# The last attention written out head by head, its projection inside, and maxima passes over four key segments of 256

## The reference

```
qkv  = x @ qkv_w + qkv_b                       # 12 heads of 16 channels, 2 images: 24 heads in all
attn = (q * scale) @ k.T + rel_h + rel_w       # 2304 x 2304 scores per head
out  = softmax(attn) @ v
return out @ proj_w + proj_b
```

## Time and profile before

| | us |
|---|---|
| median of 3 runs | 4721.52 (4720.76 to 4724.44) |
| the profiled execution, its own time | 4717.87 |
| its span in the profile | 4716.0 |
| PE, PE weight loads, DVE, ACT, POOL busy | 3464.0, 1758.2, 3572.9, 2692.4, 1536.5 |
| first and last score of the last attention start | 3309.2 and 4642.6 |
| first maxima pass | 3245.9 |
| first projection matmul | 4678.7 |

### The profile page before, as it was taken

One profiled execution on the slowest core, in us unless ns is written; L12 is line 12 of the kernel. 1 busy time (PEld: TensorE's weight loads), 2 busy tenths in 40 slices (PEclk: granted clock), 3 DMA queues, 4 the chain that ended last, 5 costly groups with the idle time before them and its releaser, 6 DMA issues. The chain is left out here.

```text
span 4716.0 us, 120406 instructions
## 1 busy us (share of the span) xinstructions
PE 3464.0 (73%) x47313; PEld 1758.2 (37%) x47313; DVE 3572.9 (76%) x3605; ACT 2692.4 (57%) x4414; POOL 1536.5 (33%) x1124
## 2 busy tenths in 40 slices
PE   3898764148777756306777775765999999999996
PEld 2476622012222223101222222451566665666563
DVE  2755455869999936677999993555888888888884
ACT  0366617735555532864545542141888888888883
POOL 0122200059999920007999990000000000000000
PEclk8899977558888878656878887865999999999998
DMA  3433212432222220232222212133112222211213
GB/s 85 97 68 65 39 42 62 120 94 68 61 65 68 57 66 17 89 118 76 71 61 63 65 48 64 59 120 91 52 52 60 57 56 54 55 52 52 52 53 88
DMA packets 165533, 316.14 MB, mean 67 GB/s; under 512 B 71035, under 2 KB 110147, under 8 KB 161392
## 3 DMA queue, kind: packets, MB, share of 16 engines
q1 hardware_dynamic: 164976, 308.38, 24.9%
HBM read 199.70 MB, written 108.02 MB: 65 GB/s over the span
## 5 line engine op out<-in xcount | busy, mean ns | idle before, releaser
L2005 DVE TENSOR_REDUCE l3a_mx<-l3a_mx 128x2 f32<-128x768 f32 x1362 | 1223.9, 951 | 201.9 <-PE l3a_mx L1909 195.5
L1981 ACT ACTIVATE l3a_p<-l3a_s 128x384 f32<-128x384 f32 x2592 | 1158.5, 491 | 159.7 <-PE l3a_s L1931 149.6
L1398 POOL TENSOR_TENSOR l_scan_sc<-l_scan_s,l_scan_repc 128x768 f32<-128x768 f32 x576 | 1032.3, 1840 | 5.8 <-DVE l_scan_s L1376 5.7
L1335 ACT ACTIVATE l_scan_da<-l_scan_da,l_scan_a 128x768 f32<-128x768 f32 x576 | 504.0, 875 | 637.0 <-PE l_scan_da L1259 636.8
L1931 PE MATMUL l3a_s<-l3a_q,l3a_k 125*32 125x384 f16 x10368 | 827.7, 327 | 3.3 <-issue 3.3
L1909 PE MATMUL l3a_mx<-l3a_k,l3a_q 124*32 124x384 f16 x10896 | 717.0, 335 | 36.3 <-DVE l3a_mx L2005 29.4
L1259 PE MATMUL l_scan_dup<-l_scan_du,l_scan_pick 96*128 96x512 bf16 (+1 forms) x1152 | 350.7, 393 | 367.4 <-DMA l_scan_dt<-l_dtp 213.3
L1943 PE MATMUL l3a_o<-l3a_p,l3a_vh 128*32 128x288 f32 x6920 | 579.5, 406 | 3.0 <-issue 2.9
L1389 POOL TENSOR_TENSOR l_scan_bup<-l_scan_dus,l_scan_repb 128x768 f32<-128x768 f32 x192 | 353.1, 1839 | 656.6 <-DMA l_scan_repc<-l_bcp 656.6
L1875 POOL TENSOR_TENSOR l3a_norm<-l3a_out,l3a_spread 128x576 f32<-128x576 f32 x25 | 35.9, 1434 | 1366.8 <-DMA l3a_spread<-l_inverses 1366.8
L1286 PE MATMUL l_scan_y<-l_scan_sc,l_scan_sum 128*32 128x256 f32 x3456 | 450.1, 475 | 10.4 <-POOL l_scan_sc L1398 10.3
(11 more groups left out here) (197 smaller groups left out, 4242.6 us busy)
## 6 DMA issues: line engine op xcount, KB each, us to landing
l3a_q<-l_qx SPq DMA_DIRECT2D x104, 486.0 KB
l_scan_du<-l_dup SPq DMA_DIRECT2D x144, 144.0 KB, 2.8
l_scan_dt<-l_dtp SPq DMA_DIRECT2D x144, 144.0 KB, 3.4
l_scan_repb<-l_bcp SPq DMA_DIRECT2D x48, 384.0 KB
l_scan_repc<-l_bcp SPq DMA_DIRECT2D x48, 384.0 KB
l3a_q<-l_hx SPq DMA_DIRECT2D x26, 288.0 KB
l_dtp<-l_prep_high_t SPq DMA_DIRECT2D x16, 432.0 KB, 3.1
l_dup<-l_prep_high_u SPq DMA_DIRECT2D x16, 432.0 KB, 3.1
```

The lines of the kernel that those rows point to most:

```text
L1335: act.activation(da_ps[st % 2][:, 0:TC], da_ps[st % 2][:, 0:TC], ACT.Exp, scale=A[:, column:column + 1]).then_inc(exped, 1)
L1398: pool.tensor_tensor(SC[:, st % NSC, :], S[:, n, :], REPC[k % 2][:], ALU.mult).then_inc(weighted, 1)
L1981: act.activation(P[:, k % NP, third * SW:(third + 1) * SW], s_ps[g % NS_PS][:, 0:SW], ACT.Exp)\
L2005: dve.tensor_reduce(MX[:, h % NB, qt, 2 * pair:2 * pair + 2], mx_ps[bank][:, :, 0:RG], AX_X, ALU.max)\
```

## The change

In words, part by part:

1. **Written out.** The loop of 2 rounds of 12 heads becomes 24 heads written out on all engines, with constant waits. No passes and no loads are made for heads beyond the 24th, so the last 132 units carry no maxima passes. The dummy values before the loop and the dummy head in the drams go.
2. **Passes of 1024 columns.** The keys are cut into 9 segments of 256 (SEG), a query tile has 9, a head 162. A pass takes four segments (PER), which fill both banks, so a head has 41 passes (40 of 1024 columns and one of 512). `runs` splits a pass into matmul groups wherever the bank, the query tile or the queries' variant changes: 135 groups of four matmuls a head (27 of 512 columns, 36 of 384, 36 of 256, 36 of 128) in place of 108 of 384. One reduce gives 4 numbers per query.
3. **Placing.** Pass m stands at unit floor(m x 108 / 41) - 132, so one every 2.63 units, evenly. `join` and `turn` follow the head's last pass by 1 and 3 passes. The turn is a plain f32 matmul with the identity.
4. **SP's queue.** Keys of head h+2 are loaded ahead of the sums' stores (at unit 2); stores for head h-1 stand in head h's part as before; the inverses are stored ahead of the second queries' load.
5. **Projection inside.** Its weights are loaded at the start, three of its four operand parts in heads 7, 13 and 22, the fourth after the last head. 20 pieces (5 per image and half of the channels; 4 of 512 columns and one of 256) follow the last values on PE in the maxima's PSUM banks, DVE adds, SP stores. The scope change between attention and projection goes.

The diff, cut to its core:

```diff
-    LEAD = 160
-    HPB = 12
     NB = 3
-    NI = BH // HPB
-    CYC = 2 * THIRDS
+    NU = BH * UPH
     RG = 8 * W
     NRG = L // RG
     VAR = RK // 8
-    NMX = KT * NRG // 2
+    SEG = 256
+    NSEG = L // SEG
+    PER = 2 * CH // SEG
+    NMX = -(-KT * NSEG // PER)
     NR, NS_PS, NP = 2, 3, 6
-    AHEAD, JOIN_AT, TURN_AT, INVERT_AT = 4 * CYC, 1, 3, 32
-    MX_AT = (0, 3, 4)
+    AHEAD, JOIN_LATER, TURN_LATER, INVERT_AT = 24, 1, 3, 32
+    KEYS_AT, QUERIES_AT, ROWS_AT = 2, (14, 30, 46, 56), 22
...
+        for m in range(BH * NMX + TURN_LATER + 1):
+            unit = m * UPH // NMX - UPH - AHEAD
+            h, lag = divmod(m - NMX, NMX)
+            if h >= 0 and lag == JOIN_LATER:
+                joins[len(passes)] = h
+            if h >= 0 and lag == TURN_LATER:
+                turn_of[h] = len(passes)
+                place(unit, ("turn", h))
+            if m < BH * NMX:
+                place(unit, ("mx", m))
...
+        def runs(x):
+            out = []
+            for i in range(min(PER, KT * NSEG - x * PER)):
+                qt, seg = divmod(x * PER + i, NSEG)
+                bank, col = divmod(i * SEG, CH)
+                for key in (seg * SEG, seg * SEG + SEG // 2):
+                    if out:
+                        b0, c0, q0, k0, n0 = out[-1]
+                        if (b0, q0, k0 + n0) == (bank, qt, key) and variant(k0 // RG) == variant(key // RG):
+                            out[-1] = (b0, c0, q0, k0, n0 + SEG // 2)
+                            continue
+                    out.append((bank, col + key - seg * SEG, qt, key, SEG // 2))
+            return out
...
+        operand_at = {HPC + 1: (0, 0), NH + 1: (0, 1), BH - 2: (1, 0)}
+        pieces = [(b, m, at, w) for b in range(B) for at, w in LCH for m in range(CC)]
...
+                for h in range(BH):
+                    later = h + 2
...
+                    if later < BH:
+                        sp.wait_ge(scored, h * UPH + KEYS_AT)
+                        load_keys(sp, later)
+                    if h >= 1:
+                        store_sums(sp, h - 1)
+                    queries(0)
+                    if later < BH:
+                        sp.wait_ge(scored, h * UPH + ROWS_AT)
+                        load_rows(sp, later)
+                    if h >= 1:
+                        store_inverses(sp, h - 1)
+                    queries(1)
+                    if h >= 1:
+                        store_out(sp, h - 1)
+                    queries(2)
+                    if h in operand_at:
+                        load_operand(sp, *operand_at[h])
+                    queries(3)
+                    if h + 1 < BH:
+                        load_shift(sp, h + 1)
...
-                        pe.transpose(out[0:KT, 0, 0:128], M[:], eye[:, :]).then_inc(mx_made, 1)
-                    else:
-                        qt, pair = divmod(what[1], NRG // 2)
-                        for a in range(2):
-                            g = 2 * pair + a
-                            for c in range(4):
-                                at = qt * 128 + 32 * c
-                                mm = pe.matmul(out[32 * c:32 * c + 32, a, 0:RG], Q[h % NB][0:rows, variant(g), at:at + 32],
-                                               K[h % NB][0:rows, g * RG:(g + 1) * RG], start=True, stop=True)
+                        pe.matmul(out[0:KT, 0, 0:128], M[:], eye[:, :], start=True, stop=True).then_inc(mx_made, 1)
...
+                    for bank, col, qt, key, size in runs(x):
+                        for c in range(4):
+                            at = qt * 128 + 32 * c
+                            mm = pe.matmul(out[32 * c:32 * c + 32, bank, col:col + size],
+                                           Q[h % NB][0:KROWS - 1, variant(key // RG), at:at + 32],
+                                           K[h % NB][0:KROWS - 1, key:key + size], start=True, stop=True)
+                    mm.then_inc(mx_made, 1)
...
-                with pe.Fori(0, NI) as i:
-                    for g in range(ST):
-                        score(i, g)
-                        maxima(i, g)
-                        for e, k in values_at(g):
-                            values(i, e, k)
+                for u in range(NU):
+                    score(u)
+                    for n in at_unit.get(u, []):
+                        mx_pass(n)
+                    for k in values_at(u):
+                        values(k)
+                values(BH * KPH - 1)
+
+                pe.wait_ge(w_loaded, 32)
+                pe.wait_ge(mx_taken, len(passes))
+                for n, (b, m, at, w) in enumerate(pieces):
+                    if m == 0 and at == 0:
+                        for c in range(CC):
+                            pe.wait_ge(ot_loaded[b][c], 16)
+                    since(pe, added, n - 3)
+                    for c in range(CC):
+                        mm = pe.matmul(accumulator(n)[:, 0:w], w_sb[:, c, m * CP:(m + 1) * CP],
+                                       operand(b, c)[:, at:at + w], start=c == 0, stop=c == CC - 1)
+                    mm.then_inc(projected, 1)
...
-                        dve.tensor_reduce(MX[:, h % NB, qt, 2 * pair:2 * pair + 2], mx_ps[bank][:, :, 0:RG], AX_X, ALU.max)\
+                        size = min(PER, KT * NSEG - x * PER)
+                        banks = mx_ps[n % NR][:, :, :].rearrange("p b (g k) -> p (b g) k", k=SEG)
+                        dve.tensor_reduce(MX[:, h % NB, x * PER:x * PER + size], banks[:, 0:size, :], AX_X, ALU.max)\
                            .then_inc(mx_taken, 1)
...
-            layer3_attention(nc, t, qx_dram, kx_dram, hx_dram, V, eye, ox_dram, sum_dram, inv_dram)
-        with Scope(nc, "l3o") as so:
-            OT = so.sb("ot", [CP, CC, TOK])
...
-            out_projection(nc, "l3p", X, OT, t["l3_pwT"], t["l3_pb"], CP, CC, l3_rows, out)
+            layer3_attention(nc, t, X, out, qx_dram, kx_dram, hx_dram, V, eye, ox_dram, sum_dram, inv_dram)
```

More of the change, by code:

```diff
@@ L1712, in layer3_attention @@
             s.sem(n) for n in ("scored", "exped", "summed", "o_taken", "mx_made", "mx_taken", "m_made"))
[L1713 to L1719, removed]
+        w_loaded, projected, added, x_stored = (s.sem(n) for n in ("w_loaded", "projected", "added", "x_stored"))
+        ot_loaded = [[s.sem(f"ot_loaded{b}_{c}") for c in range(CC)] for b in range(B)]
@@ L1734, in layer3_attention @@
[L1734 to L1755, removed]
+            k = u // THIRDS - 1
+            return [] if k < 0 or k % KT == 0 else [k - 1, k] if k % KT == 1 else [k]
+        def half_ended(u):
+            k, rest = divmod(u - 1, THIRDS)
+            return (k - 1) // KT if rest == THIRDS - 1 and k >= KT and (k - 1) % KT == KT - 1 else None
@@ new lines, in layer3_attention, with place @@
+        passes, at_unit = [], {}
+        turn_of, joins = {}, {}
+        def place(unit, what):
+            at_unit.setdefault(max(unit, -1), []).append(len(passes))
+            passes.append(what)
+        for m in range(BH * NMX + TURN_LATER + 1):
[8 more added lines that the diff above has]
+                place(unit, ("mx", m))
@@ L1757, in variant @@
+        joins.setdefault(turn_of[BH - 1], BH - 1)
         def variant(g):
             return max(g - (NRG - VAR), 0)
[L1760 to L1771, removed]
@@ L1945, in values @@
                     mm.then_inc(summed, 1)
-                for g in range(4):
-                    pe.matmul(o_ps[32 * g:32 * g + 32, 0:QG], VH[NB - 1][:, 0, :], P[:, 0, 0:QG], start=True, stop=False)
-                pe.wait_ge(loaded[0], LOADS)
-                pe.wait_ge(loaded[1], LOADS)
-                for number, h, pos, what in before_loop():
-                    if what[0] == "turn":
-                        pe.wait_ge(m_made, h + LEAD)
-                    mx_pass(number, h, number % NR, what)
@@ L1985, in _, with take_out @@
-                take_out(NI, -1, 1)
+                def take_out(half):
+                    h = half // NHALF
+                    act.wait_ge(summed, (half + 1) * KT)
+                    since(act, divided, h - 1)
+                    act.activation(OUT[:, h % 2, half % NHALF, :], o_ps[:, 0:QG], ACT.Copy).then_inc(o_taken, 1)
+                act.wait_ge(cleared, 2 * NB + 3)
+                for u in range(NU):
+                    k, third = divmod(u, THIRDS)
+                    act.wait_ge(scored, u + 1)
+                    if third == 0:
+                        since(act, summed, k - NP + 1)
+                    act.activation(P[:, k % NP, third * SW:(third + 1) * SW], s_ps[u % NS_PS][:, 0:SW], ACT.Exp)\
+                       .then_inc(exped, 1)
+                    half = half_ended(u)
+                    if half is not None:
+                        take_out(half)
@@ new lines, in _, with add @@
+                for n in at_unit[-1]:
+                    mx_take(n)
+                for u in range(NU):
+                    for n in at_unit.get(u, []):
+                        mx_take(n)
```

(15 more changed lines are left out.)

293 lines of the change are left out of this document (127 added, 166 removed).

## The result

The changed kernel takes 4658.94 us (median of 4 runs, 4651.62 to 4667.68) against 4721.14 for the kernel before: a ratio of 0.9869, 95% interval 0.985 to 0.9888. That is 62 us less. I had forecast 4703, 18 less, with a range that ended at 4672: the direction was right, the size was not. The profiled execution took 4656.65, its span is 4654.8.

A forecast was written before the change was run, and what follows sets the result against it. PE's streaming was taken to bound the last attention. Terms +20 - 8 - 1.5 - 3.3 + 1 - 27 gave -19 on the profiled 4717.87, so 4699, and 4703 as median; the range was 4672 to 4734.

The forecast's parts named there:

- End, -27: After the last scores: image 0's projection runs beside the loads, then one operand load of 6 us and image 1; -27 us.
- Loop, -3.3 and +1: Loop over the heads: its edge goes, -3.3 us; 9% more matmuls a head raise the other "issue" idles, +1 us.
- Placing, +20: New order of passes in the last attention: a head takes 55.5 us against 54.67, 0.87 slower; +20 us over 22.8 heads.
- (a): Pass behind the third score in two groups running: three scores stand together, 0.18 us lost three times a head, 0.54.
- (b): Half ends: PE has less work to fill the gap in ACT's exponentials; 1.10 us a head, before 0.88.
- (c): Turn: the pass behind it waits for the reduce of the pass before; 0.7 us a head, before 0.8.
- Last 132 units, -8: Last 132 units, without passes: ACT's 1.33 us a group is the bound, 44 groups; -8 us.
- rival D: Clock falls in the last stretch, PE then needs 1.96 us a group; 14 us with half the time lost, 4717; chance 0.17.
- Before unit 0, -1.5: Passes ahead of the first score: 51 of 1.20 us in place of 66 of 0.949; -1.5 us.
- SP and POOL, 0: SP's moved stores and operand loads, POOL unchanged: 0, at worst 0.5 us a head where a shift comes late.
- reduce, 0: DVE's reduce of 1024 columns takes 1.22 us; worth 0 while PE bounds, at most 1.9 us a head.
- rival A: Stalls of the placing estimate in the last attention don't come: -18 in place of +20, 4665, or 4684 if half come; chance 0.18.

The follow-up runs named there:

- outside: The changed kernel with the projection outside again, in a scope of its own after the attention: 4686.84 us, 0.9931 of the kernel before.
- all_out: The kernel before with only its loop over the heads written out on all engines: 4699.25 us, 0.9957 of the kernel before.
- split kernels: The changed kernel with its matmul runs cut to at most 256 columns (4674.0 us) or to 128 (4822.51 us).
- split128: The changed kernel with every maxima group cut into groups of 128 columns, 324 a head: 4822.51 us, 1.0206 of the kernel before.
- placed: The changed kernel with passes moved from behind a group's third score, and two moved near half ends: 4654.74 us, 0.9859 of the kernel before.
- turn_gap: The changed kernel with only the pass behind a turn placed two units later: 4642.09 us, 0.9829 of the kernel before.
- actdve_out: The kernel before with the loop over the heads written out on ACT and DVE alone: 4712.77 us, 0.998 of the kernel before.
- pe_out: The kernel before with the loop over the heads written out on PE alone: 4706.03 us, 0.9965 of the kernel before.
- inside_384: The changed kernel with passes of 768 again, each two groups of 384 placed as before: 4661.36 us, 0.9863 of the kernel before.

## Why the prediction was wrong in size

The profiled executions give -61.2, forecast -19. By its own steps:

**End, -27: right.** 28.6 in the profile, 27.9 by `outside`, one load of 6.1 where I had taken 6 from bounds of 4.3 and 17.

**Loop, -3.3 and +1: wrong, the largest miss.** I had left 22 us over as "issue" idles, tied only the 3.3 at the edge to the loop, and charged more for denser matmuls. 19 to 22 were the loop's: -19.4 in the scores' span of `all_out` and -22 in its median, of which PE's stream alone is -14.2 and -15. I did not ask what else in PE's stream the change takes away: the branch, and in front of each wait a register instruction. Why PE runs dry is settled in part: the idles lie at every 256th instruction of its code, in the loop, in the split kernels and in the first attention alike. Why blocks come late in the loop at 44.8 instructions per us, and not written out at 45.9, stays open; no run kept the loop on PE and took only its register instructions away. The Trainium skill, "Runtime: NRT & Kernel Launch", section "Instruction fetch mechanics", says that a branch to code not yet fetched stalls and that fetching is otherwise mostly hidden. The edge's idle of 3.25 us agrees. That it is mostly hidden agrees with after and all_out, where PE has no such idle, but not with `split128`, where 165 us are lost at these places without a branch.

**Placing, +20: right in kind, +5.7 in size.** The heads came out 0.25 longer, not 0.87. Of the 1.64 for (a) and (b) 54.92 - 53.2 - 0.74 = 0.98 came. The walk used 0.44 per exponential and 0.51 from score to exponential. They are 0.393 and 0.39, which makes both stalls shorter. But that the 0.98 is (a) and (b) is not shown: `placed` does away with (a) and puts a pass into the gap of (b), PE's waits for ACT shrink, and a head is no shorter. What holds it at 54.9 there stays open. Term (c) was right: 0.74 of idle, forecast 0.7, and `turn_gap` gives it back nearly whole, 0.82 a head.

**Last 132 units, -8: mis-sized by the same price.** The last 124 scores take 50.0 us (turn at 4560.0 to 4610.0), against 124/108 x 54.67 = 62.8 at the old pace: -12.8. ACT is busy 66.77 of 70 and the clock stays 1.00, so rival D did not occur.

**Before unit 0, -1.5: mis-sized, by the clock.** -4.4, since a pass takes 1.13 and not 1.20 there:

```profile
3248.36 47.62 DVE L2042 TENSOR_REDUCE l3a_mx<-l3a_mx 128x4 f32<-128x1024 f32 x42 [40.95 <-PE l3a_mx L1938]
```

My 1.20 came from a cycle in which PE at half clock and DVE wait for each other, as before. The same 40 us, of before and then of after:

```profile
3256.00:3296.00 40.00, 35.06 (x340) 5.79 (x336) 38.55 (x43) 0.00 (x0) 0.00 (x0) 0.50 0.00 1
3256.00:3296.00 40.00, 21.56 (x468) 8.25 (x460) 39.87 (x36) 0.00 (x0) 0.00 (x0) 1.00 0.01 1
```

The clock is full after, PE is busy for half of the time, and DVE alone sets the pace. In a stretch of 30 us there the granted clock was 0.50 in all five kernels with passes of 768 and 0.84 to 1.00 in all eight with passes of 1024.

Together, in the profiled executions: -28.6 end, -19.4 loop, -12.8 last stretch, -4.4 before unit 0, +1.4 for a first pass that starts later, +5.7 heads: -58.1 of -61.2. The other 3 are not placed. One sum of the prediction is a little off: 0.88 and 0.8 are 1.68, not the 1.75 of stalls that they were to explain, which is under 2 us over 24 heads.

**SP and POOL, 0; reduce, 0: right.** A head is no longer by their waits.

**The range.** It reached down to rival A's 4672 and no further, since no bound held a gain for the 19 us of "issue" idles that I could not place. With them at -19 the lower end would have been 4653, and 4658.94 in the range. A itself did not happen: the turns are 54.92 apart, not under 54, and 0.98 of its 1.64 came after all.

## What to carry to other kernels

Idles that a sum leaves unexplained belong in the range, and the first question is which of them the edit could take away; where engines run a long loop, one run with the loop written out on one engine alone prices it there. An idle that stands at every 256th instruction of an engine belongs to its code and not to what it waits for, and numbering the instructions in the trace shows that without a run. Read an engine's price from where a queue stands before it (here 49 in a row), never from rows where each waits for its input. A pass that must wait for another engine's result is better placed a little later: two units were worth 17 us here.

## What the runs showed of the hardware that I had not expected

- ACT's hand-over from PE: the idle before an exponential is 0.16 us where it waits against constants and 0.24 in the loop. It goes by ACT's own waits, not PE's. ACT's timeline in `actdve_out`, where PE is still in the loop, and in `pe_out`, where ACT is:

```profile
3901.80 2.80 ACT L1981 ACTIVATE l3a_p<-l3a_s 128x384 f32<-128x384 f32 x6 [0.16 <-PE l3a_s L1931]
```
```profile
3901.97 2.72 ACT L1981 ACTIVATE l3a_p<-l3a_s 128x384 f32<-128x384 f32 x6 [0.24 <-PE l3a_s L1931]
```

- Exponentials of 384 columns have a record of 0.49 each and follow each other every 0.393, 0.404 with registers.
- PE's "issue" idles lie on a grid of 256 instructions in every kernel that has them, but for the one in the projection, where PE waits for the operand load. Written out, at 42 instructions per us there are none in `all_out` and one of 1.2 us in `inside_384`, at 46 none in after, at 55 10 us, at 64 103.
- Matmuls of 128 columns to different column groups start 14.7 to 17.3 ns apart.
- The clock stayed full in the last stretch (1.00 from 4540 to 4610), though there PE no longer has maxima to do. Before unit 0 it was 0.50 with PE's records at 35.06 of 40 us, and 1.00 with them at 21.56 of 40.
